# Expert stage: the loop over rounds of six blocks written out on ScalarE

## The reference

```
x = x + mamba2(gate0(x))
x = x + ffn0(gate1(x))          # this part
x = x + attention(gate2(x))
x = x + ffn1(gate3(x))

def ffn0(x):                    # 2048 tokens of 512, E = 8 experts, top 2
    top_vals, top_idx = top_k(x @ gate_w.T + gate_b, 2)
    routing = softmax(top_vals)
    for e in range(E):
        h = x @ w1[e].T + b1[e]
        x_glu, x_lin = h[:, 0::2], h[:, 1::2]
        y = x_glu * sigmoid(1.702 * x_glu) * (x_lin + 1.0)
        ye = y @ w2[e].T + b2[e]
        out = out + ye * sum(routing * (top_idx == e))[:, None]
    return out
```

## Time and profile before

| | us |
|---|---|
| median of 3 runs | 2553.23 (2552.86 to 2554.62) |
| the profiled execution, its own time | 2547.29 |
| its span, first to last instruction | 2545.6 |
| expert stage, from the first round on ScalarE to the last block's store | 828.5 to 1263 |

### The profile page before, as it was taken

The page is one execution under the profiler, slowest core; times in us unless marked ns, Lnnn a source line. Parts: engine busy times, 40 slices in busy tenths (PEclk is TensorE's granted clock), DMA queues, the critical chain, the costliest instruction groups (busy, mean ns, idle before and its releaser), DMA issues.

```text
span 2545.6 us, 34103 instructions
## 1 busy us (share of the span) xinstructions
PE 2254.4 (89%) x10411; PEld 1662.3 (65%) x10428; DVE 1854.1 (73%) x2831; ACT 1002.1 (39%) x2076; POOL 675.5 (27%) x544
## 2 busy tenths in 40 slices
PE   0789989989897899788878999999999988999998
PEld 0344444444455777567667888888888876788886
DVE  8989898889888755665555668768777785666665
ACT  3243342342442544454434444444434444322222
POOL 5434434343332433434331012121212210000000
PEclk9999999999999899899989999999999998999999
DMA  5000001010025422343251000010010101000001
GB/s 208 17 33 34 33 17 50 17 37 29 32 84 197 171 96 67 139 153 126 88 177 34 1 33 17 17 38 21 17 38 21 50 17 50 25 25 25 25 12 66
DMA packets 52802, 148.62 MB, mean 58 GB/s; under 512 B 5008, under 2 KB 5008, under 8 KB 48336
## 3 DMA queue, kind: packets, MB, share of 16 engines
q1 hardware_dynamic: 34144, 96.08, 10.5%
q10 hardware_dynamic: 12864, 32.81, 3.5%
q0 software_dynamic: 5680, 18.62, 2.4%
HBM read 113.14 MB, written 34.34 MB: 58 GB/s over the span
## 4 chain that ended last, share of the span: by engine, by line
PE 39%; issue 30%; POOL 10%; DVE 8%; POOLq 6%; ACT 4%; ACTq 1%; DMA 1%; DVEq 0%; SPq 0%
PE bank L342 9%; PE bank L344 9%; PE bank L343 9%; PE bank L2347 3%; PE bank L2398 2%; PE bank L2400 2%; PE bank L2399 2%; POOLq L497 2%; POOL g_v L505 2%; POOL g_v L498 2%; POOLq L520 1%; POOLq L523 1%; POOL g_s L519 1%; PE bank L2462 1%; POOLq L509 1%
## 5 line engine op out<-in xcount | busy, mean ns | idle before, releaser
L2222 PE MATMUL bank<-um,w_in 128*128 128x512 f32 x576 | 262.4, 609 | 3.3 <-DVE lm L1566 3.2
L2222 PEld LDWEIGHTS bank<-um,w_in 128*128 128x128 f32 x576 | 109.5, 195 | 134.8 <-issue 127.8
L342 PE MATMUL bank<-u_hi,aw_hi 128*128 (+1 forms) x384 | 157.7, 411 | 12.6 <-DVE u_lo L1963 8.9
L1186 ACT ACTIVATE probs<-bank,nmx 128x128 f32<-128x128 f32 (+3 forms) x256 | 131.5, 526 | 91.8 <-DVE nmx L1986 91.8
L1193 ACT ACTIVATE pt_hi<-bank 128x512 fp32r<-128x512 f32 (+1 forms) x192 | 93.9, 526 | 161.7 <-PE bank L2347 161.7
L344 PE MATMUL bank<-u_hi,aw_lo 128*128 (+1 forms) x384 | 151.4, 394 | 0.0
L343 PE MATMUL bank<-u_lo,aw_hi 128*128 (+1 forms) x384 | 151.2, 394 | 0.0
L2001 DVE TENSOR_TENSOR pt_lo<-bank,pt_hi 128x512 fp32r<-128x512 f32 (+1 forms) x192 | 108.6, 593 | 40.4 <-ACT pt_hi L1193 38.5
L2398 PE MATMUL bank<-mw,bu_hi 128*128 (+1 forms) x312 | 127.5, 409 | 11.7 <-DVE mw L1850 6.6
L342 PE MATMUL bank<-u_hi,fw_hi 128*128 128x512 f32 x352 | 136.9, 389 | 0.0
L343 PE MATMUL bank<-u_lo,fw_hi 128*128 128x512 f32 x352 | 136.9, 389 | 0.0
(11 more groups left out here) (387 smaller groups left out, 6203.2 us busy)
## 6 DMA issues: line engine op xcount, KB each, us to landing
m_stage<-in_moe SPq DMA_DIRECT2D x21, 1024.0 KB, 6.7
y_slot<-m_o ACTq DMA_DIRECT2D x39, 256.0 KB, 2.1
g_v<-in_fT SPq DMA_DIRECT2D x18, 512.0 KB, 3.5
gates<-g_v SPq DMA_DIRECT2D x18, 512.0 KB, 2.8
f_stage<-in_ffn SPq DMA_DIRECT2D x11, 768.0 KB, 4.3
u_g<-gates SPq DMA_DIRECT2D x8, 1024.0 KB, 8.6
aw_in<-in_att SPq DMA_DIRECT2D x4, 1280.0 KB, 6.0
w_in<-in_w_in ACTq DMA_DIRECT2D x1, 4640.0 KB, 16.8
```

The source lines that it names most:

```text
L342: nc.tensor.matmul(out, hi_w, hi_x, start=start, stop=False)
L1186: A(probs[:, h % 2, PR_AT[qb]:PR_AT[qb] + w], S_[bk][:, c0:c0 + w], ACT.Exp, bias=nmx[:, h % 2, qb:qb + 1], scale=SCALE, accum_out=rsum[:, ...
L2222: mm = M(dst[:], w_in[:, k, c0:c0 + P], um[:, k, :], start=(k == 0), stop=(k == KC - 1))
```

## The change

One line: on ScalarE, and there alone, the hardware loop over rounds becomes a Python loop, so that six rounds stand one behind the other in the program. `pair` is then a number when the program is built and no register. The register arithmetic that came from it (semaphore counts, table addresses, the address of the store) goes; the loads of `flag`, `e` and the bias rows from the table stay, and so do the Ifs on them.

```diff
@@ -1100,7 +1100,7 @@
             u_hi_copy(1)
             gate(moe_pair(0), 0)
             gate(moe_pair(0), 1)
-            with act.Fori(0, NBLK // 6) as pair:
+            for pair in range(NBLK // 6):
                 nxt = next_expert(pair * 6, False)
                 packed = [packed_of(pair * 6 + i, False) for i in range(3)]
                 for h in range(2):
```

## The result

The changed kernel takes 2525.85 us (median of 4 runs, 2524.34 to 2527.89). The kernel before, beside it, takes 2553.05 (4 runs, 2547.46 to 2554.62). By these medians it is 27.2 us faster. The ratio, which is estimated apart from the medians, is 0.9878 with a 95% interval of 0.9838 to 0.9917, so anything from 21 to 41 us. Forecast were 31.5 us faster, and a range of 2513 to 2538.

What follows compares the result with a forecast made beforehand. TensorE's work was taken to bound the expert stage, ScalarE counting only where TensorE waits. 12.4 + 5.7 + 9.7 + 4.4 + 1.3 - 2 = 31.5 us off 2553.23 gave 2521.7, said as 2522; range 2513 to 2538.

Steps and rivals of the forecast that it cites:

- What bounds the kernel: Expert stage: TensorE's own work sets the time; ScalarE matters only where TensorE waits for it.
- The gap is the branch: ScalarE's turns: 2.78 us behind the branch back, 5.10 at the fourth, read as code fetched again; goes with the branch.
- The rival that the gap would move with the first load: ScalarE's turns: the gap belongs to something else, such as the first table load, so almost nothing is gained; 2552, chance 0.05.
- The turns' waits: TensorE's `by_lo` waits at five turns: 12.4 us saved at first, second and fifth, 6.7 at fourth, 4.4 at third.
- the low bound of 3.8 us: ScalarE, each turn: least saving, 7.3 us at the first turn against 3.5 at the loop's end; 4.4 was taken.
- The clock behind them: TensorE after the three turns without expert change: no 1.2 GHz stretch, 5.7 us saved; at the fourth turn 3.0 more.
- The rest (1.3 us): Loop start and six expert changes within rounds: fewer register instructions before `by_hi`, 0.15 to 0.25 us each, 1.3 us.
- Code fetched once, straight on: ScalarE's six written-out rounds: 1981 instructions, about 15 pieces of 8 KB, to come in while it works.
- the slower rival: ScalarE stops at each new code piece, 15 times at 2.8 us; with all 15, 33 us slower, 2586; chance 0.05.
- The give-back: Block 2, where `by_lo` has no room: small fetch gaps at new places cost 0.4 us a round, 2 us (0 to 10).
- a sign against itself: Blocks 1 and 2: the prediction called itself wrong if TensorE waits for `by_lo` there.
- VectorE or the clock takes part of it back: Block 2: VectorE's gate scans become last, TensorE idles 1 to 2 us in five rounds, or clock gain lost; 2530, chance 0.14.

Runs made afterwards that it cites:

- far-jump kernel: Changed kernel plus, behind each of the first five rounds, an always-taken forward branch on ScalarE over 400 never-run instructions: 2542.93 us, one run.

## Why the prediction was right, and where it was off

**What bounds the kernel: right.** The time went where TensorE's waits were, and ScalarE's own busy time over the stage did not change (187.43 and 188.00 us).

**The gap is the branch: right.** Gone at all five turns, kept where turns were kept, and made again by a far jump forward. The rival that the gap would move with the first load would have left 2.78 us at 898.6; there are none. The Trainium skill's 108 ns (Advanced Engine Details and Errata, Control Flow Timing), from which that rival had its 0.1 us a turn, is a figure for the branch itself, whose record is 0.05 us here. What comes behind it depends on where its target is.

**The turns' waits: right in size, and in part by luck.** Said were 12.4 + 6.7 + 4.4 = 23.5 us. Measured: 27.2 - 3.69 = 23.5, with the third turn at 3.69 where 3.6 had been said. `by_lo` was to be done at 902.9 at the first turn, and TensorE took its transposes at 903.38 without a wait. The fourth turn's 6.7 rested on two gaps of 6.4 us in one profile, which were 5.8 in the next of the same kernel; with that pair the five waits fell from 26.6 to 3.69, by 22.9. And the low bound of 3.8 us would not have taken the first wait whole: 907.26 - 3.8 = 903.46 is 0.2 behind 903.28.

**The clock behind them: right as a mechanism.** It is 1.00 in both quiet rounds. TensorE's busy time fell by 7.4 us where 5.7 + 3.0 = 8.7 had been said, and by 9.2 with GpSimd's order changed.

**The rest (1.3 us): seen at one place.** The first round, where the start of the loop is the only part, went from 53.62 to 52.09 us, but the kernel before took 52.94 in another execution, and the changed one 52.86. Of the six changes of expert one shows it: TensorE's wait at 1094.89 is 1.08 us in every profile in which the loop stays, and 0.64 to 0.67 in every one in which it is written out.

**Code fetched once, straight on: almost free.** No gap of 1 us stands in ScalarE's queue where a turn was, so the slower rival did not come. What there is are stretches of 0.3 to 0.45 us behind the If of nine blocks (L1054), as the prediction had allowed. The 1981 instructions for the six rounds should be 2941 - 1412 + 388 = 1917, which are 15 pieces of 128 all the same, and one packet or none of them came in at each former turn.

**The give-back: the step that was mis-sized.** I gave back 0.4 us a round, 2 in all, because `by_lo` of block 2 had no room. It was 5.4 us of new idle time in the stage. The place was right, since these are the waits in blocks 1 and 2 that the prediction named as a sign against itself, but the reason was not. I had looked at VectorE alone, as if its work would shift with ScalarE's and keep its length. What I left out was GpSimd, whose additions hang on its own gathers and shifted by 2.2 us where VectorE shifted by 5.2. Ordering them one gather earlier gave 7.4 us (the median) or 5.7 (the stage, 390.8 to 385.1). With that edit in both kernels the change gives 30.8 us by medians and 29.5 by the stage (414.65 to 385.12), close to the 31.5 of the sum.

**The sum.** By the stage the gain is 23.5 + 7.4 - 5.4 = 25.5 us and not 31.5. Of the 6.0 us between them, 3.4 are the give-back beyond its 2, 1.3 the clock, and 1.3 the rest, which can't be told apart from the new idle time. The rival "VectorE or the clock takes part of it back" had 1 to 2 us a round in five rounds, and it was about one. By the stage alone the time would be 2553.2 - 25.5 = 2527.7, between the forecast's upper end (2527) and that rival's lower one (2528). That the first median fell inside the forecast is therefore worth little: the second pair, 23.4 us apart by medians, would have fallen outside, at 2529.8. The ends given for the terms, 2518 to 2540, don't come out of the bounds as they are said either; added up they are some 2519 to 2541.

The rows that would have told me stood in the trace of before. GpSimd's additions end at 918.75, VectorE's scans begin at 919.94, so there were 1.2 us between them, and the change moves VectorE by more than 4. The Trainium skill, SBUF — State Buffer, SBUF: two separate sides, says that VectorE and GpSimd share one pair of ports, that it is locked for a whole instruction, and that it also bears on a VectorE operation with two inputs in that memory against one of GpSimd that reads there. The rows agree in the main: the scan, recorded 0.8 us behind the start of the first addition, takes 1.6 us longer, and the copy recorded inside the scan ends with it. The second addition, though, is recorded from 0.4 us behind the start of the scan and takes its usual 1.30 us, so the order of the recorded starts is not the order in which the two took their turn.

## What to carry to other kernels

When a stall on one engine goes, list the other engines' work in the stretch behind it and ask of each whether it moves along. What is queued behind something with a pace of its own (here gathers, 4 us apart) moves less, and its overlaps change. A loop on an engine can cost a gap at each turn when its body is long (388 and 295 instructions on ScalarE here); writing it out is worth it only where the engine that bounds the kernel waits for it, which the timeline of that engine tells and the gap itself does not. If a loop must stay, the place of its first instruction can matter too.

## What the runs showed of the hardware that I had not expected

- A taken branch to code far away costs ScalarE 2.7 to 3.2 us in the expert stage, and 3.6 to 5.6 while 1 MB weight pieces are under way; at the turns of the attention loop it is 3.3 to 3.5. Behind a jump over 30 instructions there are at most 0.38 us. VectorE's loop has 261 instructions by the same count as ScalarE's 388 and 295, and its turn takes 0.3 us (897.83 to 898.09 in the kernel before); both of ScalarE's stall. Where between 30 and 295 ScalarE's stall begins is not shown.
- With the loop's first instruction just ahead of the end of a piece of code, by my count, there is a second gap of 1.0 to 1.3 us, and of 2.2 in two profiles beside the weight pieces. Eight idle instructions ahead of the loop took it away.
- A pair of scans on VectorE that meets two additions on GpSimd takes 3.94 us and not 2.33, and a 0.19 us copy on GpSimd that meets the scans takes 1.13.
- Behind waits of 4.1 us TensorE's granted clock fell to the 1.2 GHz level in all quiet rounds of the kernel before (a mean of 0.97 over the round in one profile, 0.94 in the next). Behind waits of 2.3 to 2.9 us it sometimes did and sometimes did not: in the far-jump kernel round 2 (2.27 us) ran at 1.00 and round 3 (2.33 us) at 0.97.
